# Latent attention with stacked split products, straight code and a longer software pipeline

## What is computed

```python
kv_c = x @ W_kvd + b_kvd                      # 64 wide
keys_c, values = heads(kv_c @ W_ku + b_ku), heads(kv_c @ W_vu + b_vu)
keys_r = rope(heads(kv_c @ W_kr + b_kr))
q_c = x @ W_qd + b_qd                         # 192 wide
queries_c = heads(q_c @ W_qu + b_qu)          # 16 heads of 128
queries_r = rope(heads(q_c @ W_qr + b_qr))    # 16 heads of 64
scores = concat(queries_c, queries_r) @ concat(keys_c, keys_r).T / sqrt(192), causal
ctx = softmax(scores) @ values
x = x + (ctx @ W_o + b_o)
```

## Time and profile before

| | us |
|---|---|
| median of 3 runs (1715.1 to 1719.35) | 1716.51 |
| the profiled execution, its own time | 1717.53 |
| its span, first to last instruction | 1715.2 |
| PE busy | 1561.6 (91%) |
| DVE busy | 1402.8 (82%) |
| ACT busy | 1122.1 (65%) |
| POOL busy | 746.5 (44%) |
| mean granted TensorE clock | 0.959 of full speed |

### The profile page before, as it was taken

How to read it: one execution, slowest core, us unless ns; L and a number is a source line. 1 busy time by engine, 2 the same in 40 slices (tenths; PEclk the granted TensorE clock), 3 DMA queues, 4 the chain that set the end, 5 groups by cost and what they waited for, 6 DMA issues and landing times. The chain is left out here.

```text
span 1715.2 us, 45769 instructions
## 1 busy us (share of the span) xinstructions
PE 1561.6 (91%) x18290; PEld 1320.9 (77%) x18290; DVE 1402.8 (82%) x2513; ACT 1122.1 (65%) x2171; POOL 746.5 (44%) x727
## 2 busy tenths in 40 slices
PE   5899999998746999999999999999999999999455
PEld 5888888887535888888888888888888888888234
DVE  3788777787375889889899899898898898898687
ACT  3565555565344777777777777777777777777474
POOL 1566555565144344434434434444344354343014
PEclk9999999999677999999999999999999999999777
DMA  6000000000041111111111111111111111110001
GB/s 192 2 1 2 2 2 0 1 1 0 1 147 46 49 41 50 50 50 49 50 46 43 49 50 50 49 50 50 43 51 44 50 49 50 50 50 2 1 11 33
DMA packets 41613, 66.69 MB, mean 39 GB/s; under 512 B 7749, under 2 KB 40194, under 8 KB 41282
## 3 DMA queue, kind: packets, MB, share of 16 engines
q1 hardware_dynamic: 41410, 63.93, 12.9%
HBM read 62.08 MB, written 1.84 MB: 37 GB/s over the span
## 5 line engine op out<-in xcount | busy, mean ns | idle before, releaser
L1144 POOL TENSOR_TENSOR xa_CW<-xa_CTX,xa_CH 128x500 fp32r<-128x500 f32 x187 | 305.4, 1633 | 592.6 <-ACT xa_CH L1338 592.6
L1366 DVE TENSOR_TENSOR xl_ACC<-xl_ACC,xl_PB 125x896 f32<-125x896 f32 x320 | 438.3, 1370 | 11.0
L1330 ACT ACTIVATE xl_PB<-banks,xl_BIB,xl_SCB 125x896 f32<-125x896 f32 x384 | 401.0, 1095 | 32.1 <-PE banks L1202 31.7
L1357 DVE TENSOR_SCALAR xl_PB<-xl_PB 125x896 f32<-125x896 f32 x384 | 249.6, 650 | 64.1 <-ACT xl_PB L1330 63.0
L1312 ACT ACTIVATE xl_V<-banks 125x256 f32<-125x256 f32 x384 | 147.4, 384 | 155.3 <-PE banks L1169 155.3
L1169 PE MATMUL banks<-xa_WVhigh,xa_CH 128*125 128x256 f32 x768 | 238.6, 311 | 0.0
L1169 PE MATMUL banks<-xa_WVlow,xa_CH 128*125 128x256 f32 x768 | 216.0, 281 | 0.0
L1169 PE MATMUL banks<-xa_WVhigh,xa_CW 128*125 128x256 f32 x768 | 215.9, 281 | 0.0
L1303 ACT ACTIVATE xl_KXhigh<-banks,xa_bk 128x500 fp32r<-128x500 f32 x192 | 130.4, 679 | 100.4 <-PE banks L1169 100.4
L1218 PE MATMUL banks<-xl_PB,xl_V 125*32 125x112 f32 x6144 | 187.2, 262 | 1.5 <-DVE xl_PB L1357 1.5
L1373 DVE SCALAR_TENSOR_TENSOR xl_KXlow<-banks,xa_bk,xl_KXhigh 128x500 fp32r<-128x500 f32 x192 | 137.4, 715 | 55.0 <-ACT xl_KXhigh L1303 54.4
(11 more groups left out here) (234 smaller groups left out, 3954.6 us busy)
## 6 DMA issues: line engine op xcount, KB each, us to landing
xa_CTX<-in_ctxT SPq DMA_DIRECT2D x93, 500.0 KB, 3.6
fw_WO<-in_W_o SPq DMA_DIRECT2D x1, 2048.0 KB, 17.7
xq_WR<-in_w_gating SPq DMA_DIRECT2D x1, 2048.0 KB, 9.7
X<-in_x SPq DMA_DIRECT2D x1, 1792.0 KB, 10.2
out<-ff_R SPq DMA_DIRECT2D x16, 112.0 KB, 1.9
fw_QUT<-in_W_quT SPq DMA_DIRECT2D x1, 1536.0 KB, 12.5
xa_CTX<-in_ctxT SPq DMA_DIRECT2D x1, 1500.0 KB, 15.0
xq_WL<-in_w_linear SPq DMA_DIRECT2D x1, 1024.0 KB, 11.8
```

The lines of the kernel that those rows point to most:

```text
L1144: nc.gpsimd.tensor_tensor(context_piece(CW, i), context_piece(CTX, i), context_piece(CH, i), ALU.subtract).then_inc(ctx_low, 1)
L1330: nc.scalar.activation(PB[t % PR][:, :, :], banks[0:TK, 2 * i:2 * i + KT, 0:QW], ACT.Exp, scale=SCB[j][:, t:t + 1], bias=BIB[j][:, t:t + 1 ...
L1357: nc.vector.tensor_scalar(pt, pt, E_HI, E_LO, ALU.min, ALU.max).then_inc(clipped, 1)
L1366: nc.vector.tensor_tensor(ACC[j][:, :, :], prev[:, :, :], PB[t % PR][:, :, :], ALU.add).then_inc(summed, 1)
```

## The change

- **Stacking.** The 64 upper query rows and 64 key rows no longer share a tile. Weights are loaded twice, into rows 0 to 63 and 64 to 127, and the latent is kept as CS: high part in its upper 64 rows and low part in its lower 64. One matmul then gives high times high plus low times high. A query tile takes 5 matmuls, a key tile 2, a unit 19. The latents of a round need three projections instead of two; ACT makes 6 copies in place of 4, DVE 3 low parts in place of 2 (two of them of 64 rows). W_quT is 256 columns wide, and there are 5 more loads.
- **Straight code.** The loop over rounds is gone; every round is written out.
- **Pipeline.** Transposes of the unit before stand at a unit's end on PE, values are those of two units before and stand between tiles 0 and 1, the output product stands ahead of tile 3 in k2 and k6. ACT takes the turned probabilities of two units before as a unit's first instruction. DVE's residual stands in k2 and k6, its statistics in k3 and k7, and the aggregate goes straight to its place (no copy, line 727). The wait for POOL ahead of the scores of k0 is for two of its units instead of all.

```diff
@@ fold_weights: loads
-                sp.dma_start(WD[:, :, QC:H], d["W_kvd"].rearrange("(k p) n -> p k n", p=P)).then_inc(attn_in, 16)
+                sp.dma_start(WD[:, :, QC:2 * P], d["W_qd"][:, P:QC].rearrange("(k p) n -> p k n", p=P)).then_inc(attn_in, 16)
+                for at in (2 * P, 2 * P + KVC):
+                    sp.dma_start(WD[:, :, at:at + KVC], d["W_kvd"].rearrange("(k p) n -> p k n", p=P)).then_inc(attn_in, 16)
...
-                sp.wait_ge(zeroed, 3)
-                for b in range(2):
-                    sp.dma_start(by_two[1][0:QC - P, :, b, b * RD:(b + 1) * RD], wqr[P:QC, :, b, :]).then_inc(attn_in, 16)
-                sp.dma_start(KRW[P - KVC:P, :], d["W_kr"]).then_inc(attn_in, 16)
+                for rows in (slice(0, KVC), slice(KVC, P)):
+                    for b in range(2):
+                        sp.dma_start(by_two[1][rows, :, b, b * RD:(b + 1) * RD], wqr[P:QC, :, b, :]).then_inc(attn_in, 16)
+                    sp.dma_start(KRW[rows, :], d["W_kr"]).then_inc(attn_in, 16)
@@ latent_loop: products
-                    for n, i in enumerate(tiles):
+                    if first_rows is not None:
                         for a, c in ((0, 0), (0, 1), (1, 0)):
-                            mm = nc.tensor.matmul(dst, stationary(a, i), moving(c, i), start=(n == 0 and a == c),
-                                                  stop=(n == len(tiles) - 1 and a == 1))
+                            nc.tensor.matmul(dst, first_rows(a), CP[c][:, :], start=(a == c), stop=False)
+                    for a in range(2):
+                        mm = nc.tensor.matmul(dst, stacked(a), CS[:, k, :], start=(first_rows is None and a == 0), stop=(a == 1))
@@ latent_loop: PE, the whole order of a unit
+                for r, k, u, project in steps(3):
+                    first = r == 0
+                    if project and k == 0:
+                        project_latents(r, first)
+                    if known(u):
+                        if u:
+                            pe.wait_ge(s_masked, u)
+                        if k < QUADS:
+                            pe.wait_ge(rope_ready, (r - 1) * 2 * NH + 8 * (k + 1))
+                            pe.wait_ge(abs_ready, (r - 1) * NH + 4 * (k + 1))
+                            pe.wait_ge(kabs_ready, (r - 1) * 4 + 2 * (k // 2) + 2)
+                        scores(u)
+                    if project:
+                        if k == 0:
+                            pe.wait_ge(c_read, r * C_READS + 3)
+                            pe.wait_ge(c_low, r * C_LOWS + 3)
+                        if k == 1:
+                            pe.wait_ge(c_read, r * C_READS + C_READS)
+                            token_rows(r, first)
+                        tile(r, k, 0, first)
+                    if known(u - 2):
+                        values(u - 2)
+                    if project:
+                        tile(r, k, 1, first)
+                        tile(r, k, 2, first)
+                    if known(u - 3) and (u - 3) % QUADS == QUADS - 1:
+                        output(u - 3)
+                    if project:
+                        tile(r, k, 3, first)
+                        tile(r, k, 4, first)
+                    if known(u - 1):
+                        transposes(u - 1)
@@ latent_loop: ACT, the order of a unit
+                for r, k, u, project in steps(2):
+                    if known(u - 2):
+                        turned(u - 2)
+                    if project:
+                        if k == 0:
+                            act.wait_ge(c_done, r * 2 + 1)
+                            copy_latents(CP[0][:, :], 0)
+                            act.wait_ge(c_done, r * 2 + 2)
+                            copy_latents(CS[:, 0, :], 1)
+                            copy_latents(CS[:, 1, :], 2)
...
+                        latent_half(r, k, 0)
+                        latent_half(r, k, 1)
+                    if known(u):
+                        probabilities(u)
```

More of the change, by code:

```diff
@@ L337, in _ @@
                 for j in range(QUADS):
-                    for i, rows in enumerate((slice(0, P), slice(P, QC))):
+                    for i, rows in enumerate((slice(0, P), slice(P, 2 * P))):
                         if j:
@@ L399, in latent_loop @@
         C = [sb(f"C{i}", [P, NR]) for i in range(2)]
-        CP = [[sb(f"C{i}{part}", [P, NR], F32R) for i in range(2)] for part in ("high", "low")]
+        CP = [sb(f"C0{part}", [P, NR], F32R) for part in ("high", "low")]
+        CS = sb("CS", [P, 2, NR], F32R)
         Q = [sb(f"Q{i}", [P, NH, NR]) for i in range(2)]
@@ L404, in latent_loop @@
         KR = [sb(f"KR{i}", [P, NR]) for i in range(2)]
-        KV = [sb(f"KV{i}", [T, PPR, KVC]) for i in range(2)]
+        KV = [sb(f"KV{i}", [T, PPR, KVC]) for i in range(3)]
         CQ = [sb(f"CQ{i}", [T, PPR, NH]) for i in range(2)]
@@ L427, in latent_loop, with steps, known, c_tile @@
         z_done, z_ready, o_done, o_read, x_added = (sem(s) for s in ("z_done", "z_ready", "o_done", "o_read", "x_added"))
-        def rounds(eng, body):
-            body(0, 0, True, False, False)
-            body(1, 1, True, True, False)
-            with eng.Fori(1, ROUNDS // 2) as i:
-                body(i * 2, 0, True, True, True)
-                body(i * 2 + 1, 1, True, True, True)
-            body(ROUNDS, 0, False, True, True)
+        def steps(behind):
+            for n in range(UNITS + ALL + behind):
+                r, k = divmod(n, UNITS)
+                yield r, k, n - UNITS, r < ROUNDS
+        def known(u):
+            return 0 <= u < ALL
+        def c_tile(m):
+            return bank[0][:, 0:NR] if m == 0 else bank[1][:, (m - 1) * NR:m * NR]
         def rope_rows(h):
@@ L472, in await_bank @@
                     if at < 2:
[L473 to L474 removed]
+                        pe.wait_ge(c_read, old * C_READS + (4 if at == 0 else C_READS))
+                        pe.wait_ge(c_low, old * C_LOWS + (1 if at == 0 else C_LOWS))
                         return
@@ L523, in scores, with transposes @@
                         h = 4 * j + q
-                        mm = nc.tensor.matmul(bank[S_BANK][0:T, q * T:(q + 1) * T], Q[1 - par][:, h, p * T:(p + 1) * T],
-                                              K[1 - par][:, h, p * T:(p + 1) * T], start=True, stop=True)
+                        mm = nc.tensor.matmul(bank[S_BANK][0:T, q * T:(q + 1) * T], Q[par][:, h, p * T:(p + 1) * T],
+                                              K[par][:, h, p * T:(p + 1) * T], start=True, stop=True)
                     mm.then_inc(s_done, 1)
-                def transposes(u, k):
+                def transposes(u):
@@ L536, in values @@
                     pe.wait_ge(pt_ready, u + 1)
+                    if u:
+                        pe.wait_ge(z_ready, u)
                     for half in range(2):
                         mm = nc.tensor.matmul(bank[Z_BANK][half * KVC:(half + 1) * KVC, 0:2 * T],
-                                              KV[par][:, k // QUADS, :], PT[k % 2][:, half::2, :], start=True, stop=True)
+                                              KV[(u // UNITS) % 3][:, u % UNITS // QUADS, :], PT[u % 2][:, half::2, :], start=True, stop=True)
@@ L540, in values, with output @@
                     mm.then_inc(z_done, 1)
-                def output(u, p):
+                def output(u):
+                    pair = u // QUADS
                     pe.wait_ge(z_ready, u + 1)
+                    if pair:
+                        pe.wait_ge(o_read, pair)
                     for m in range(NH // 2):
-                        mm = nc.tensor.matmul(bank[O_BANK][0:T, 0:H], ZZ[p][:, m, :], WVO[:, m, :],
+                        mm = nc.tensor.matmul(bank[O_BANK][0:T, 0:H], ZZ[pair % 2][:, m, :], WVO[:, m, :],
```

379 lines of the change are left out of this document (146 added, 233 removed).

## The result

The changed kernel takes **1702.03 us** (median of 5 runs, 1701.85 to 1707.56), the kernel before 1716.51 in the same session (1714.99 to 1719.35). The ratio is 0.9919, its 95% interval 0.9902 to 0.9936: faster by 0.8%, 14.5 us by the medians. The forecast was 1711 and faster by 5.9. The sign is right, and so is the chain of work in the rounds. The time lies at the very end of the stated range of 1702 to 1720, 0.03 us inside it, and the gain is two and a half times the forecast. By the number alone it is nearer to rival 2 (1697) than to the forecast; what rules rival 2 out is the trace.

A forecast was written before the change was run, and what follows sets the result against it. Bound: a ring of DVE and POOL, not PE. Head +4.95, round 1 +0.5, rounds 2 to 6 -6.4, round 7 -2.2, tail -2.5, statistics copy +0.2: -5.9 us, from 1716.5 to 1711; range 1702 to 1720.

The forecast's parts named there:

- rival 2: Ordinary units shrink from 4.85 to 4.44 us, the full maximum being held by PE's load, not POOL; 1697 us, chance 0.11.
- The bound: Ordinary units of the rounds: closed by DVE and POOL at 4.85 us, not by PE, and staying there.
- the ring: Ordinary unit's closed chain: reciprocal, POOL's probabilities and key additions, full maximum, DVE's offset, sines and values, next reciprocal; 4.85 us.
- Part 1, products: Five fewer products save PE 0.55 us a unit, but hidden behind DVE and POOL, bringing nothing in ordinary units.
- Part 2, the order: Values wait for ACT's turning, so units with an output last 8.3 us; a plain round takes 48.6 us against 48.9.
- Rival 1, the hidden output: PE uses its lead, so 13 outputs stop costing 2.4 us of DVE's waiting; 1680 us, chance 0.09.
- Part 3, straight code: Rounds 3 to 6: without the loop's two turns, 4.9 us go, half of it a clock effect.
- Rival 4: The loop's turns did not cause the 4.9 us, or straight code stalls elsewhere; 1716 us, no difference, chance 0.14.
- Part 4: Rounds summed: round 1 +0.5 us, rounds 2 to 6 -6.4, round 7 -2.2.
- Part 5, the tail: Round 8: five units gain 1.0 us each, two with an output lose about 1.2; -2.5, ends -6 and +4.
- Part 6, the head: Before the rounds: five more loads and larger weights delay the start; with round 0, +4.95 us together, load bounds 3 and 7.
- Rival 3, the clock: PE, less busy, drops to a lower clock at each round's start; 1723 us, up to 1729, chance 0.14.

The follow-up runs named there:

- e6: The changed kernel with POOL's keys' additions of the unit before moved ahead of the probabilities; 4.8 us less between first and last mask.
- e7: The changed kernel without the full maximum and the offset instruction, scale and mask applied in one operation; 17.5 us less between first and last mask.
- e3: The changed kernel without stacking (24 products, two latent tiles, 16 loads), straight code and new order kept; 1695.7 us, ratio 0.9879.
- e1: The kernel before with only its loop over rounds 2 to 7 written out; level with the kernel before, rounds 3 to 6 at 195.9 us for 200.5.
- e2: The changed kernel with the old order of steps; stacking, straight code and the shorter wait of k0's scores stay; ratio 0.9989 to the kernel before.
- e4: The changed kernel with the output product's eight matmuls split, two in each unit instead of eight in every fourth; 1677.5 us.
- e8: The changed kernel with DVE's two bias copies waiting only for their own two loads, not all 21; first mask at 80.7 us for 84.7.

## Why the prediction was right, and where it was off

- **The bound.** Right, and shown. The units without an output product stay at 4.85 us though PE lost 0.55 us in each; e6 moves the end of the ring, e7 takes it out. Rival 2 (a full maximum that goes with PE's load) is out: the load fell and the units did not shrink, and in e3, with the higher load, they take 4.86 to 4.92.
- **Part 1, products.** Right for those units; between first and last mask stacking gains 2.4 us with the new order (e3). With the old order no run has it by itself: from e1 to e2 6.9 us go, 3.3 in rounds 2 to 6 and 4.1 in round 7, but e2 also has scores of k0 that don't wait for all of POOL's round. In round 7 that is most of it, since its last unit takes 4.91 us for 8.45, the latter with the clock's fall of e1 in it.
- **Part 2, the order.** The mechanism holds link by link: the turning right behind the exponentials, the values right behind it, the output at 1.97 us after the reciprocal (2.15 forecast), the residual at 5.62 (5.8), DVE's wait 2.30 (2.4), the forecasts in brackets; each of these is a little too long. Units came out from mask to mask as 5.04, 4.88, 8.03, 4.86, 4.92, 4.85, 8.03 and 7.09, where the prediction had 5.1, 5.05, 8.3, 4.85, 4.95, 4.85, 8.3 and 7.2: 0.9 us a round, and over rounds 2 to 6 the 4.4 us between the -6.4 forecast and -10.8 measured (249.4 to 238.6). This is the largest miss of the sum: a plain round was to gain 0.3 us and gained 1.2. By the runs the 10.8 are 4.6 to 4.7 from before to e1 (straight code), 3.3 from e1 to e2 (stacking and the shorter wait of k0) and 3.0 from e2 to the changed kernel (the order). Rival 1, the hidden output, did not come; e4 shows that the wait can be taken away, by cutting the product and not by more lead.
- **Part 3, straight code.** The 4.9 us were 4.6 in the rounds, but e1 gives them back in rounds 1, 7 and 8. Whether they are gone for good in the changed kernel isn't shown: no run has it with the loop. Rival 4 was nearer to the truth for this part alone than its chance of 0.14 says.
- **Part 4.** Round 1 +0.5 forecast and measured; round 7 -2.2 and -3.2.
- **Part 5, the tail.** This is the other term that was mis-sized: -2.5 forecast, -6.4 measured (53.6 to 47.2), beyond the -6 that was its lower end. Units without an output gained 0.9 each, near the 1.0 of the text (five of 3.80 us on the mean, 3.45 to 4.24, against 4.66, 3.95 to 5.16), but those with one lost nothing: 6.45 and 6.29 against 6.53 and 6.22, where +1.2 each was forecast. The clock has a share in this that no run separates: its mean was 0.78 for 0.68. The last mask to the end of attention gained another 2.1.
- **Part 6, the head.** +4.95 forecast, +3.6 measured in this pair. Four more kernels with the same 21 loads have the first mask at 85.4 to 86.9, three with 16 loads at 76.4 to 80.4, so by the means (86.1 of five, 79.2 of four with the kernel before) the term is 6.9, inside the bounds of 3 to 7 and 2 us above the value taken. Three of the five had a stretch at the lower clock in round 0 (see the last section); without them the mean is 85.1 and the term 5.9. That the measured pair had only 3.6 is luck, and it makes the miss of the sum larger. The head is the change's one real loss, and e8 takes 4 us of it back.
- **Rival 3, the clock.** Did not come: the granted clock is 1.00 in all windows of rounds 1 to 7 of the changed kernel, with PE standing still for 4.7 us a round. In other kernels single stretches of 3.4 us at the lower clock were seen, in round 0 (e2, e6 and e7) and at the start of round 1 (e1), but at no other round's start up to round 7.

Sum of the misses: rounds -4.4, round 7 -1.0, tail -3.9, head -1.3, 10.6 in all; from the -5.9 forecast to the -16.2 of the spans it is 10.3. No term had the wrong sign, but all four misses go the same way, so that nothing cancelled, and the range just held.

## What to carry to other kernels

An engine that is 95% busy (PE in a plain round before) needn't be the bound: follow the longest run of an engine's rows without a gap, and ask of each instruction that is too long for its size who ends at the same time. Taking work off an engine pays only once the waits around it are gone: stacking was worth 2.4 us beside the ring and the lumped output product, 9.6 with the product spread and 15.9 with the ring cut as well, from the very same edit, and at the head it cost 5.7, 9.0 and 5.9 us in the same three pairs. Before moving a long operation further down a pipeline, try cutting it into the pieces in which its inputs arrive.

## What the runs showed of the hardware

- An accumulation of eight matmuls in one bank can be spread over four units, with all other matmuls of three units in other banks in between, at no price that shows: in e4 a piece takes 0.68 us from its start to that of the next product (214.66 to 215.34 in one unit), so 2.7 for four, while the whole product takes 3.27 (164.38 to 167.65 in the changed kernel).
- The granted clock in the drain differed between orders of the same work: from the last round's first mask to its last it is 0.71 with the old order (e2), 0.79 in the changed kernel and 1.00 with the output product spread (e4). A drain that is costed at one clock, as in part 5, can be off by that.
- Where the rounds start differs under one and the same head: the first mask of the five kernels with 21 loads and no change at the head lies between 84.7 and 86.9 us, one profiled execution each. A difference of 2 us there can't be read from one pair of profiles. The clock goes with it. In e2, e6 and e7 (86.7, 86.6 and 86.9) it was at the lower level for 3.4 us in round 0, from 60.5 on, and in the changed kernel and e4 (84.7 and 85.4) it was not. The window in e2:

```profile
60.40:63.90 3.50, 3.50 (x20) 3.50 (x19) 2.12 (x5) 1.92 (x4) 0.65 (x1) 0.52 0.02 5
```

- In e4 the residual's addition to X, two SBUF inputs, took 0.72 us on the mean where it took 0.42 in the changed kernel; it had come to run beside POOL's additions. A gap closed in one place moved an instruction under the same exclusion as the full maximum.
- The offset instruction, also with two SBUF inputs (ll_MC and ll_CQS) but of another kind, is held in the same way when it falls beside POOL. It takes 0.16 us in 63 of 64 units of the changed kernel, and 0.87 once, at the start of round 8, where POOL's probabilities run from 415.33 to 416.27 (DVE, then POOL):

```profile
415.42 0.87 DVE L700 SCALAR_TENSOR_TENSOR ll_NM<-ll_MC,ll_CQS 112x4 f32<-112x4 f32 x1
```

```profile
415.33 0.93 POOL L790 TENSOR_TENSOR ll_PN<-ll_PE,ll_RI 112x448 f32<-112x448 f32 x1
```

- Not all of a held instruction comes behind POOL's end. The full maximum, 0.16 us by itself, ends 0.02 us behind POOL, and the addition to X in e4, 0.42 by itself, 0.29 behind it (189.87 to 190.59, POOL's first addition ending at 190.30). In both cases some 0.14 us of the instruction's own length lie before POOL's end. This is worked out from POOL's recorded ends, which are the rougher ones.
